# GpSimd clears 128x512 numbers of an unread buffer behind each late row scatter and each output scatter

## What is computed

```python
flat = _rmsnorm(x, ln2_w).reshape(-1, Cx)
probs = softmax(flat @ router_w.T); tp, ti = top_k(probs, 2)
tp = tp / (sum(tp) + 1e-09)
for e in range(8):
    hh = silu(flat @ w1[e].T) * (flat @ w3[e].T)      # 128 -> 341
    out = out + weights[:, e:e+1] * (hh @ w2[e].T)    # 341 -> 128
return x + out
```

## Time and profile before

| What | us |
|---|---|
| Median of three runs (lowest and highest) | 612.19 (610.11 to 612.92) |
| Span of the profiled execution, first to last instruction | 610.4 |
| PE busy | 501.5 (82%) |
| DVE busy | 429.3 (70%) |
| ACT busy | 314.3 (51%) |
| GpSimd busy | 254.2 (42%) |
| GpSimd, 32 row scatters (L1052) | 31.8 |
| GpSimd, 39 output scatters (L1059, three groups) | 25.7 + 15.9 + 2.5 |

### The profile page before, as it was taken

One profiled execution on the slowest core, in us unless ns is written; L12 is line 12 of the kernel. 1 busy time (PEld: TensorE's weight loads), 2 busy tenths in 40 slices (PEclk: granted clock), 3 DMA queues, 4 the chain that ended last, 5 costly groups with the idle time before them and its releaser, 6 DMA issues.

```text
span 610.4 us, 11302 instructions
## 1 busy us (share of the span) xinstructions
PE 501.5 (82%) x3819; PEld 281.4 (46%) x3819; DVE 429.3 (70%) x1065; ACT 314.3 (51%) x522; POOL 254.2 (42%) x275
## 2 busy tenths in 40 slices
PE   2999986699999799996776888998969657498880
PEld 1533334477777445443322432333412157397770
DVE  6898838888999925757786896999752038166564
ACT  0787985869999001201254453764745334166661
POOL 3000005133436401102364895997353632555562
PEclk9999995999999799999578789999989859599996
DMA  8999954100139250110233522003035447389925
GB/s 302 409 421 422 405 189 149 42 19 20 34 129 411 85 109 0 39 26 15 68 110 99 157 72 60 2 1 104 35 129 177 176 121 222 112 277 384 324 89 175
DMA packets 39570, 93.43 MB, mean 153 GB/s; under 512 B 7488, under 2 KB 24944, under 8 KB 35168
## 3 DMA queue, kind: packets, MB, share of 16 engines
q1 hardware_dynamic: 35072, 86.96, 40.6%
q0 software_dynamic: 2272, 4.69, 2.2%
q10 hardware_dynamic: 2176, 1.13, 0.6%
HBM read 69.39 MB, written 21.00 MB: 148 GB/s over the span
## 4 chain that ended last, share of the span: by engine, by line
PE 54%; DVE 21%; ACT 7%; issue 6%; another core or an unknown queue 5%; DMA 4%; POOL 1%; SPq 1%; DVEq 0%; POOLq 0%; ACTq 0%
PE ps L1578 8%; DVE A L2385 7%; PE ps L1755 6%; PE ps L1489 6%; PE ps L1506 6%; PE ps L1404 5%; PE ps L1859 3%; PE ps L1656 3%; PE ps L1747 3%; DMA R<-in_adj_in 3%; PE ps L1842 2%; PE ps L1603 2%; PE ps L1381 1%; DVE bst L1916 1%
## 5 line engine op out<-in xcount | busy, mean ns | idle before, releaser
L2385 DVE TENSOR_REDUCE A<-ps 128x1 f32<-128x512 f32 (+3 forms) x160 | 86.3, 601 | 13.7 <-PE ps L1656 13.0
L1302 ACT ACTIVATE A<-ps 128x1024 f32<-128x1024 f32 (+3 forms) x80 | 68.4, 894 | 49.2 <-PE ps L1747 40.3
L1007 POOL TENSOR_TENSOR G<-G,A 128x1024 f32<-128x1024 f32 (+3 forms) x40 | 73.8, 1888 | 9.1 <-ACT A L1302 8.9
L1656 PE MATMUL ps<-A 96*128 96x512 f16 (+3 forms) x160 | 55.4, 388 | 10.4 <-DVE A L2385 5.1
L1578 PE MATMUL ps<-A,G 128*128 128x512 f32 x128 | 62.1, 611 | 0.0
L1404 PE MATMUL ps<-R,G 128*128 128x512 f32 x128 | 59.2, 605 | 1.0 <-DVE G L1959 0.8
L1859 PE MATMUL ps<-A 128*128 128x128 f16 (+1 forms) x702 | 50.3, 228 | 6.0 <-issue 6.0
L1506 PE MATMUL ps<-R 128*128 128x128 f16 x768 | 48.2, 219 | 6.7 <-DVE x L2077 5.8
L1506 PEld LDWEIGHTS ps<-R 128*128 128x128 f16 x768 | 45.3, 98 | 14.3 <-issue 6.6
L1747 PE MATMUL ps<-A 97*128 97x512 f16 (+3 forms) x160 | 45.2, 366 | 6.9 <-ACT A L1302 5.1
L2059 DVE SCALAR_TENSOR_TENSOR R<-R 128x512 f16<-128x512 f32 x64 | 46.7, 754 | 5.0 <-ACT R L1157 4.7
(11 more groups left out here) (311 smaller groups left out, 933.0 us busy)
## 6 DMA issues: line engine op xcount, KB each, us to landing
A<-w_split SPq DMA_DIRECT2D x39, 533.0 KB
A<-in_adj_t SPq DMA_DIRECT2D x16, 1024.0 KB, 17.5
slots_in<-xn SPq DMA_DIRECT2D x1, 8320.0 KB, 22.4
R<-in_adj_in SPq DMA_DIRECT2D x7, 1024.0 KB, 6.1
w_split<-A SPq DMA_DIRECT2D x9, 725.0 KB, 4.1
xn<-in_adj_in SPq DMA_DIRECT2D x5, 1024.0 KB
xT<-in_adj_in SPq DMA_DIRECT2D x4, 1024.0 KB
A<-in_f_w SPq DMA_DIRECT2D x16, 170.5 KB
```

The lines of the kernel that those rows point to most:

```text
L1007: pool.tensor_tensor(total, total, probabilities(n, pair)[:, :, t0:CW], ALU.add).then_inc(s_sum, 1)
L1302: act.activation(probabilities(n, pair)[:, :, t0:CW], ps[:, 2 * pair:2 * pair + 2, t0:CW], ACT.Exp, scale=1.0 / (SQ * SQ * float(HD) ** 0. ...
L1656: last = pe.matmul(ps[:, bank, 0:width], queries(t // TPC, h)[0:KQ, P * (t % TPC):P * (t % TPC) + P], keys(b, h // (NH // NKV))[0:KQ, 0:wi ...
L2385: dve.reduce_max(pm[:, h, t % TPC, b:b + 1], ps[:, bank, 0:width], AX_X).then_inc(s_rmf, 1)
```

## The change

In the stage above, GpSimd gets a memset of `xT[:, 0:512]` (128 partitions of 512 numbers) behind each of the eight late row scatters and behind each output scatter but the last: 46 memsets. Each is put through `chain`, so GpSimd waits until it is done before it takes the next scatter. The values are not read by anything.

```diff
+        unused = xT[:, 0:CW]
...
             pool.wait_ge(s_route, ROUTE_BASE[2] + POSITIONED)
+            def pause():
+
+                chain(pool.memset(unused, 0.0))
+
             for t in range(GTS[2]):
                 for which in range(2):
                     scatter_rows(2, t, which)
+                    pause()
             for n in range(SLOTS):
                 scatter_output(n)
+                if n + 1 < SLOTS:
+                    pause()
```

## The result

| | before | after |
|---|---|---|
| median of the runs | 611.75 us (610.11 to 612.92, 4 runs) | 629.83 us (627.50 to 631.24, 4 runs) |
| span of the profiled execution | 610.4 us | 625.7 us (its time 627.5) |
| first late row scatter starts | 513.86 us | 510.75 us |
| from there to the end of the span | 96.5 us | 114.9 us |
| ACT's last copy of an output starts | 597.3 us | 581.3 us |

The account below looks back on a forecast made before the run. GpSimd was taken to become the bound: 46 periods of 2.40 us after 513.86 put the last scatter at 624.3; 9.6 us behind it and 1.8 from span to median give 635.7 us, range 627 to 645.

Parts of the forecast that it names:

- the period: GpSimd's time from one late scatter to the next: 1.06 + 0.03 + 0.53 + 0.78 = 2.40 us, above 1.89.
- the tail: From the last scatter's start to the end of the span: landing, load, additions, store, 9.6 us.
- the restart: From the memset's end to the next scatter on GpSimd: 0.78 us, because the sequencer prepares the scatter only after the wait.
- GpSimd as the bound: In the last 97 us GpSimd needs 2.40 us per scatter, above 1.89, so no scatter waits for ACT any more.
- Sign (1): In the changed profile, ACT never releases GpSimd after the first late row scatter; scatters start every 2.3 to 2.5 us.
- Sign (3): In the changed profile, the last scatter starts near 624 us, and 9 to 10 us follow.
- The pauses pay: Rival: scatters restart 0.09 us behind the memset, period 1.71 us, other engines' stalls gone, time 603.9 us (-1.4%); chance 4%.
- The preparation is hidden: Rival: the sequencer prepares the next scatter during the memset, 0.30 us remain, period 1.92, time 613.6 us (+0.2%); chance 6%.
- Scatters that alternate with memsets are dear: Rival: all scatters cost 1.31 us or the restart over 0.78; period 2.68 or above, time 648.6 us or more; chance 8%.
- Late rows: The eighth late row scatter starts at 530.7 instead of 522.97 us; PE may wait a few us, with over 20 in hand.
- The pace to compare with: 1.89 us per scatter on average before, taken as the pace of PE, ACT and DVE; above it GpSimd becomes the bound.
- The other engines' gain: PE, ACT and DVE finish the last slot some 9 us earlier from the first stall alone; none of it reaches the end.

Follow-up runs that it names:

- the kernel with hidden preparation: Against the changed kernel: the same 46 memsets, in two places by turns, each waiting only for the memset two before it; 600.34 us, ratio 0.9865.

## Why the prediction was right, point by point

The predicted 635.7 us are 5.9 us over the median of 629.83 and 8.2 us over the 627.5 of the profiled execution, of which there are rows. 3.1 of them are the earlier start at 510.75, which no row of before could tell; 4.2 are the period, 46 x (2.40 - 2.308); 0.8 are the tail, 8.8 us instead of 9.6. Set against the start of the first late row scatter the forecast was 23.5 us, the measured lengthening 18.4, and 4.2 + 0.8 are the difference.

- *The period.* The term that was mis-sized is the scatter: 0.98 us, not 1.06. The prediction took the scatter behind a copy and the one that stood alone as the nearest, but all scatters behind a memset except two take as long as those in the run without waits, the low bound of 0.97. The memset (0.54 against 0.53 estimated from half of a 1024-wide one and from a 512-wide one) and the restart (0.78 to 0.81 against 0.78) were right; the step from scatter to memset takes 0.01 us or less instead of 0.03. The errors add up and don't cancel: only the memset and the restart, short by 0.01 us each, err the other way.
- *The restart.* This was the deciding term, and two runs show it: hiding it (0.78 to 0.17) turned a loss of 18.4 us into a gain of 8.6 with the same memsets, and taking the memset away but not the wait left it at 0.80. The Trainium skill's 50 ns for the sequencer's dispatch (page "DMA: Bandwidth & Descriptors", section "Anatomy of one DMA — SWDGE (gpsimd) path") would have led to an estimated period of 1.76 us; the trace doesn't agree, 2.308 was measured.
- *GpSimd as the bound.* Right: a second memset lengthened the stretch by 22.2 us, 46 times what it added to the period. Sign (1) was met in its period, 2.31 us, but not in its wording: the profile names ACT as releaser of 12 scatters, all with the idle time of those behind a memset, and the output scatters among them start over 19.6 us behind their own copies. Sign (3) was missed: the last scatter starts at 616.93 and not near 624, and 8.8 us follow.
- *The rivals.* "The pauses pay" named the right condition, a period below 1.89 us with the stalls gone, and the kernel with hidden preparation is that case: 1.72 on average and 600.3 us, where 1.71 and 603.9 had been worked out. Only its premise didn't hold for the change as it is. "The preparation is hidden" took 0.30 us as what is left; it is 0.17. "Scatters that alternate with memsets are dear" falls: they cost as little as those in the run without waits.
- *Late rows.* The eighth row scatter started 16.4 us behind the first (16.8 predicted); PE waited twice for rows, 3.1 us in all, hidden as foreseen. It also waited three times for weights, 3.7 us in all, which the prediction has nowhere; they are hidden too.
- *The pace to compare with.* The prediction took 1.89 us as the pace of PE, ACT and DVE alone. It held GpSimd's own effect: with the scatters spread out and their preparation hidden, ACT's last copy starts 66.6 us behind the first row scatter instead of 83.4. As the change's period lies above 1.89, this didn't touch the forecast.
- *The other engines' gain.* 12.9 us instead of "some 9 from the first stall alone", since the two-slot stalls later went too, in spite of the new waits for rows and weights. As predicted none of it reaches the end.

## What to carry to other kernels

What an instruction put between two indirect scatters costs on GpSimd isn't its own length: a wait that stops the sequencer ahead of the scatter lays the scatter's preparation bare, 0.6 us more here than the same memset with a wait two steps back. Compare the engine's new period with the pace of the work that feeds it: here a period above that pace was paid for in every step, and one below it cost nothing. The pace isn't fixed, though: here it held stalls that went when the scatters were spread out. When engines stall for nothing that the profile names, look for what another engine does without a pause in the same stretch; spreading it out can pay even if it adds work.

## What the runs showed of the hardware

- *Scatters close together hold up PE, ACT and DVE.* With 0.60 us or less between two of GpSimd's indirect scatters these engines fall behind; from 0.65 us on they don't in the 15 us of the table. With pauses behind the row scatters alone, PE issued one matmul, once two, every 0.7 us or more from 534.5 to 541 us, inside a group that waits for nothing, while the DMA engines were 47% busy (535 to 540); in the kernel before these were 15% busy from 525 to 530 us. ACT stood idle for 12.36 us with all that it waits for over. What holds the engines up is open: no run here could change the scatter's own length, so whether the pause between scatters counts or their rate (one per 1.58 us held PE up, one per 1.63 didn't) isn't settled, nor whether the descriptors, the semaphores or the instruction supply is the place. The Trainium skill, page "SBUF — State Buffer", section "Who interferes with whom", says that only the port pair that DVE and GpSimd share makes engines contend, and lists none of it for PE or ACT. By that rule the port doesn't explain their rows; no run here tests it.
- *The clock goes with it.* In the kernel before the granted clock is 0.50, the lower level of 1.2 GHz, from 525 to 530 us, behind PE's idle time; in the changed kernel it is 1.00 in the same stretch, and 0.66 from 540 to 545, behind its waits for late rows and weights.
- *Sizes.* A scatter of 128 rows takes 0.97 or 0.98 us of GpSimd behind a chained memset of any length, in all but two to six of 46; with overlapped memsets of 512 columns single ones took up to 1.48. The idle time ahead of it is 0.78 to 0.81 us behind a wait, 0.30 behind another scatter that needs no wait, and 0.16 to 0.19 where the sequencer could prepare it during the memset or before. A memset of 128 partitions takes 0.11 us for 1 column, 0.22 for 128, 0.33 for 256, 0.43 for 384, 0.49 for 448 and 0.54 for 512, and a second one in a row adds 0.46.
